# Slot scores of a gated-slot attention: one float32r pass over stacked split operands in place of two float32 half passes

## The chip, the cores and the metric

The kernel runs on one core of a Trainium2 chip. Its engines are TensorE (PE, matrix products; PEld is its weight load), VectorE (DVE), ScalarE (ACT), GpSimd (POOL) and SyncE (SP, which issues the transfers). The metric is device time in microseconds (us) of one execution.

## What is computed

A layer of four parts over x of shape 4 x 256 x 256 in float32: a causal attention, a feed-forward with int8 quantization, a second attention with 64 slots per head, and the feed-forward again, each on a layer norm of x and added to x. The change is in the second attention (16 heads, 128 wide). Its part that matters here:

```python
s = hs @ Ws1.T @ Ws2.T + bs2                # Ws1 16 x 256, Ws2 1024 x 16: rank 16
s = jnp.clip(s, -CLAMP, CLAMP).reshape(B, T, H, M).transpose(0, 2, 1, 3)
z = jax.lax.cumlogsumexp(s, axis=2)
es = jnp.exp(s)
enz = jnp.exp(-z)
...
A = jnp.where(mask, jnp.einsum('bhtd,bhjd->bhtj', q, k) * scale, 0.0)
ok = enz * jnp.einsum('bhtj,bhjm->bhtm', A, es)
qv = jax.nn.softmax(ok, axis=-1)
W2 = jnp.where(mask, jnp.einsum('bhtm,bhjm->bhtj', qv * enz, es), 0.0)
o = jnp.einsum('bhtj,bhjd->bhtd', W2, v)
```

## The kernel before

Each engine has its own program, written out by hand in the order in which it runs; semaphores (`wait_ge`, `then_inc`) tie them together, and an engine that waits holds up everything behind it in its program. The 1,024 tokens are four batches `b` of 256 (two tiles of 128). Heads go in eight pairs.

Products that need more than one rounded pass are split: a float32 operand becomes a float32r head (`_hi`, copied by ACT) and the float32r rest (`_lo`, subtracted by DVE or POOL), and three float32r passes take the place of a float32 product, which PE runs as two half passes. In the trace each half pass is a row of its own.

The scores of the slots come in two steps. At the head of the second attention `s1_product(b)` multiplies the 16 rows of Ws1 with the normalized tokens of batch `b` in float32, and ACT (`s1_copy`) brings the result out of PSUM into `s1`: 16 rows, with a row of ones at row 32 written by DVE (`BIAS_ROW`). Then there is one task "s" for each pair of heads and each half of the tokens, 16 in all: four products of `s1` (128 tokens as stationary operand) with 128 columns of `ws2` (16 rows of Ws2 and the bias in row 32). DVE clips the result (`b_clip_s`), ACT takes the exponential, and a sum over the tokens, a reciprocal and the later products follow.

The other tasks of a half are the projections q0, q1, k0, k1, the prefix sum z, the value and gate chunks c0 to c3, and the transposes et. In the loop (`b_body`, one pass per pair, four batches in each) PE puts them between the steps of the attention. For an even batch the order on PE is: transposes of the normalized slot weights `qp` (line 1554), task "s" (line 1453), W2 product (lines 1520 and 1523), q0, and so on. ACT, in the same place, runs the value copy and the tanh of chunk c3 (lines 697, 698), then copies the transposed weights to `zT` (line 727), on which the W2 product waits (`b_z`).

The second attention starts with a head part outside the loop. There DVE runs, one after the other: layer norm scaling of x, the two `tail`s that split x, the quantization of feed-forward tile 2 (`ffn_quant`: range, then rounding), the scaling of tile 3 and its quantization, the clip of the first slot scores, and more. PE runs in that part: transposes of x, `s1_product(0)` and `(1)`, the feed-forward transposes of tile 2, the first task "s". The products for batches 2 and 3 follow later in the head.

Of the kernel before, what the change touches and what calls it, by code (L numbers as in the profile page):

```python
# [38 lines left out]
P = 128  # L39
B, T, D = 4, 256, 256  # L40
HEADS = 16
# [5 lines left out]
HD = HEADS * P  # L47
M = 64
RANK = 16
BIAS_ROW = 32  # L50
SCALE = float(P) ** -0.5
MASKED = -1e10
LN_EPS = 1e-5
# [18 lines left out]
def layer_kernel(nc, x_in, a_wq, a_bq, a_wk, a_bk, a_wv, a_bv, a_wo, a_bo,  # L72
                 b_wq, b_wk, b_wv, b_wg, b_wo, b_ws1, b_ws2, b_bs2, b_gw,
                 f_w, f_ws, f_bias, consts, out):
    with ExitStack() as ctx:
# [3 lines left out]
        def sem(name):  # L79
            return ctx.enter_context(nc.semaphore(name))  # L80
# [52 lines left out]
        rinv = sb("rinv", [P, 2, 2])  # L133

        ws1 = sb("ws1", [P, C, RANK])
        s1 = sb("s1", [P, B * T])
        ws2 = sb("ws2", [P, HEADS * M])
        rot = sb("rot", [P, 2, HALF])
        rot_s = sb("rot_s", [P, 2, HALF])
        es_hi = sb("es_hi", [P, HALF], F32R)  # L140
# [3 lines left out]
        es = sb("es", [P, TILES, 2 * M])  # L144
        esT = sb("esT", [P, B * T])
        enz = sb("enz", [P, TILES, 2 * M])
        gt = sb("gt", [P, 2, 2 * P])
        G = bv_b[:, :].rearrange("p (t n) -> p t n", t=TILES)
        ok = sb("ok", [P, 2, 2, M])
# [38 lines left out]
        cast_done = sem("cast_done")  # L188
        gwh_done = sem("gwh_done")
        init_done = sem("init_done")  # L190
        ones_done = sem("ones_done")
        s1_ps, s1_done = sem("s1_ps"), sem("s1_done")
        out_st = sem("out_st")

        class Norm:
# [90 lines left out]
        def _(sp):  # L286
# [33 lines left out]
            sp.dma_start(ws1[:, :, :], b_ws1.rearrange("(c p) n -> p c n", p=P)).then_inc(small_ld, 16)  # L320
            sp.dma_start(gw[:, :], b_gw.rearrange("(p o) -> p o", o=1)).then_inc(small_ld, 16)

            sp.wait_ge(init_done, 3)
            sp.dma_start(ws2[0:RANK, :], b_ws2).then_inc(small_ld, 16)
            sp.dma_start(ws2[BIAS_ROW:BIAS_ROW + 1, :], b_bs2.rearrange("(o n) -> o n", o=1)).then_inc(small_ld, 16)
            sp.dma_start(const[:, K_TRI:K_END], consts[:, K_TRI:K_END]).then_inc(table_ld, 16)
            with sp.Fori(1, PAIRS) as i:
                cols = bass.ds(i * (2 * P), 2 * P)
# [32 lines left out]
        def _(pool):  # L361
            g = nc.gpsimd
            g.memset(minus_half[:, :], -0.5).then_inc(init_done, 1)
            g.memset(s1[:, :], 0.0).then_inc(init_done, 1)
            g.memset(ws2[:, :], 0.0).then_inc(init_done, 1)
            g.memset(wo_hi[:, :, :].bitcast(F32), 0.0)
            g.memset(wo_lo[:, :, :].bitcast(F32), 0.0)
            g.memset(oT_hi[:, 1, :, :].bitcast(F32), 0.0)
# [21 lines left out]
            def ffn_add(f, b):  # L390
# [17 lines left out]
            pool.wait_ge(bias_ld, 16 * 4)  # L408
            g.tensor_tensor(acc[:, :, :], acc[:, :, :], bo_b[:, :].unsqueeze(1).to_broadcast([P, TILES, D]), ALU.add
                            ).then_inc(a.y_acc, 1)  # L410
            with pool.Fori(0, PAIRS - 1) as i:
                split_tail(a, i + 1, 0)
                split_tail(a, i + 1, 1)
                split_out_tail(a, i, wo)
                split_tail(a, i + 1, 2)
# [103 lines left out]
        def _(act):  # L519
# [31 lines left out]

            def s1_copy(b):

                act.wait_ge(s1_ps, b + 1)
                s.activation(s1[0:RANK, b * T:(b + 1) * T], ps[0:RANK, ffns[0].banks[b], 0:T], ACT.Copy).then_inc(s1_done, 1)


            split_head(a, 0, 0)
# [79 lines left out]
            transposed(0, 2, 4)  # L638
            transposed(0, 3, 5)
            a_exp_step(0)  # L640
            act.wait_ge(small_ld, 16 * 7)
            s.activation(w8b[:, :, :], w8[:, :, :].bitcast(I8), ACT.Copy).then_inc(cast_done, 1)
            s.activation(gwh[:, :], gw[:, :], ACT.Copy, scale=0.5).then_inc(gwh_done, 1)
            with act.Fori(0, PAIRS - 1) as i:
                a_body(i, False)
            a_body(PAIRS - 1, True)
# [134 lines left out]
                        if nxt:  # L781
                            b_okexp_step(x + b + 1)

            act.wait_ge(init_done, 3)
            act.wait_ge(gwh_done, 1)
            for j, name in enumerate(B_TASKS[:-1]):
                b_task(0, 0, j, 0, 0)
# [19 lines left out]
        def _(dve):  # L807
# [19 lines left out]
            def tail(m, b, bank):  # L827

                cols = slice(b * T, (b + 1) * T)
                dve.wait_ge(xts[m].hi, b + 1)  # L830
                d.tensor_tensor(xT_lo[:, :, cols], ps[:, bank, :].rearrange("p (c t) -> p c t", c=C),
                                xT_hi[:, :, cols].bitcast(F32), ALU.subtract).then_inc(xts[m].lo, 1)

            def ffn_quant(f, b):
                ffn_range(f, b)
# [48 lines left out]
            ln_stats(0, 3, x_ld[3], 16)  # L884
            ln_scale(0, 2)
            ln_scale(0, 3)
            dve.wait_ge(init_done, 2)
            d.memset(s1[BIAS_ROW:BIAS_ROW + 1, :], 1.0).then_inc(ones_done, 1)

            def a_v(n, f, pair, half):  # L890

# [92 lines left out]
            for f in range(4):  # L984
                n = 4 + f
                a_v((n % 2, n // 2, n + 1), f, 0, 0)
                if f == 1:
                    tail(0, 2, 4)
                    a_norm_step(0)
                if f == 2:  # L990
                    tail(0, 3, 5)
            with dve.Fori(0, PAIRS - 1) as i:
                a_body(i, False)
            a_body(PAIRS - 1, True)
# [6 lines left out]
            ln_scale(1, 2)  # L1001
            tail(1, 0, ffns[0].banks[0])
            tail(1, 1, ffns[0].banks[1])
            ffn_quant(0, 2)
            ln_scale(1, 3)
            ffn_quant(0, 3)

# [191 lines left out]
            b_gate(n0(8), 0, 2, 0)  # L1199
            b_okn_max(0, 0, 0)  # L1200
            b_slots(0)
            b_recip(None, 0, 2)
            with dve.Fori(0, PAIRS - 1) as i:
                b_body(i, False)
            b_body(PAIRS - 1, True)
# [13 lines left out]
        def _(pe):  # L1219
# [34 lines left out]
            def s1_product(b):  # L1254

                pe.wait_ge(xts[1].lo, b + 1)
                for c in range(C):
                    ins = mm(ps[0:RANK, ffns[0].banks[b], 0:T], ws1[:, c, :], xT[:, c, b * T:(b + 1) * T],
                             start=(c == 0), stop=(c == C - 1))
                ins.then_inc(s1_ps, 1)  # L1260

# [164 lines left out]
            ffn_product(0, 1)  # L1426
            transpose_x(1, 0, ffns[0].banks[0])
            transpose_x(1, 1, ffns[0].banks[1])
            s1_product(0)
            s1_product(1)  # L1430
            ffn_transpose(0, 2)
            pe.wait_ge(s1_done, 2)
            pe.wait_ge(ones_done, 1)

            def b_free(i, h, j):

# [8 lines left out]
            def b_task(i, h, j, half, phase):  # L1445
                b_free(i, h, j)
                name, bank = B_TASKS[j], slot(i, h, j)[0]
                pair = i + h // 2
                n = (bank,)
                if name == "s":  # L1450
                    for t in range(HT):
                        tile = HT * half + t
                        ins = mm(PJ[bank][:, t * P:(t + 1) * P], s1[:, tile * P:(tile + 1) * P],
                                 ws2[:, bass.ds(pair * P, P)], start=True, stop=True)
                    ins.then_inc(b_.proj_ps, 1)
                elif name[0] in "qk":
                    proj_qk(b_, n, name, pair, half)
                elif name == "z":

                    pe.wait_ge(b_es_lo, phase + 1)  # L1460
                    by_tile = lambda ap: ap.rearrange("p (b t m) -> p b t m", b=2, t=2)
                    for part in (es_hi, es_lo):

                        mm(PJ[bank], sums[:, 0:P], part[:, :], start=(part is es_hi), stop=False)
                        ins = mm(by_tile(PJ[bank])[:, :, 1, :], sums[:, P:2 * P], by_tile(part[:, :])[:, :, 0, :],
                                 start=False, stop=(part is es_lo))
                    ins.then_inc(b_.proj_ps, 1)
                elif name == "et":
                    for t in range(HT):
                        ins = tr(PJ[bank][:, t * P:(t + 1) * P], es[:, HT * half + t, :], ident)  # L1470
                    ins.then_inc(b_.proj_ps, 1)
                else:

                    k = int(name[1])
                    if k == 0:
                        pe.wait_ge(b_.w_lo, pair * b_.splits + 3)
                    for c in range(C):
                        vg_chunk(bank, k, half, c)
# [230 lines left out]
```

## Time and profile before

| | |
|---|---|
| median of three runs | 822.16 us (821.42 to 823.87) |
| profiled execution | span 819.7 us from the first to the last instruction; its own time is not listed apart from the three |
| PE busy | 770.2 us, 94% of the span |
| DVE, ACT, POOL busy | 71%, 53%, 35% |
| chain that ended last | PE 90%, DVE 5% |
| the 128 half passes of the tasks "s" | 17.0 us of busy PE, mean 276 ns |

Rows of one engine overlap a little, since a matrix product is counted until its last result is out; the pace of a stream is read from the starts, or from the chain. The granted clock of PE is 1.00 at 2.4 GHz and 0.50 at 1.2 GHz.

### The profile page before, as it was taken

The page shows a single profiled execution, that of the slowest core. Times are in us where ns is not written, and L with a number is a line of the kernel's source. Part 1 is how long each engine was busy: PE and PEld are TensorE (multiplying, and loading weights), DVE is VectorE, ACT ScalarE, POOL GpSimd, SP SyncE. Part 2 cuts the span into 40 slices and gives each one's busy share as a digit, 9 for nine tenths or more (in the row PEclk, how much of TensorE's full clock was granted, in tenths as well). Part 3 has the DMA queues.
Part 4 walks back from the last instruction along what each step waited for, and adds up shares of the span by engine and source line. Part 5 has one row for each costly group of instructions (what it writes and reads, how often), then busy time and mean ns, then how long its engine had stood idle before and what let it go on. Part 6 is the DMA issues. An engine that isn't in the chain of part 4 may idle for free.

```text
span 819.7 us, 14465 instructions
## 1 busy us (share of the span) xinstructions
PE 770.2 (94%) x4556; PEld 654.7 (80%) x4556; DVE 581.3 (71%) x1502; ACT 435.4 (53%) x1188; POOL 285.7 (35%) x291
## 2 busy tenths in 40 slices
PE   5899999999999995799999999999999999999963
PEld 4788888888888883478888888888888888888852
DVE  4555555555555558878887888798879888887686
ACT  3555565555556542465556465656564665555420
POOL 6311020201102014444536346355364463553222
PEclk9999999999999999899999999999999999999997
DMA  6110101101010100100101001001010010000001
GB/s 226 40 52 13 38 13 38 51 0 51 13 38 13 51 1 14 53 0 14 54 0 54 10 13 51 0 13 51 0 33 31 13 51 0 13 0 0 1 1 52
DMA packets 23653, 23.74 MB, mean 29 GB/s; under 512 B 2369, under 2 KB 23361, under 8 KB 23506
## 3 DMA queue, kind: packets, MB, share of 16 engines
q1 hardware_dynamic: 23634, 23.51, 9.0%
q8 instruction: 10, 0.16, 0.1%
q14 instruction: 9, 0.07, 0.0%
HBM read 22.45 MB, written 1.05 MB: 29 GB/s over the span
## 4 chain that ended last, share of the span: by engine, by line
PE 90%; DVE 5%; POOL 1%; ACT 1%; issue 1%; DMA 1%; SPq 0%; DVEq 0%; ACTq 0%; POOLq 0%
PE ps L1276 22%; PE ps L1483 11%; PE ps L1385 7%; PE ps L1283 5%; PE ps L1306 5%; PE ps L1349 3%; PE ps L1390 3%; PE ps L1495 3%; PE ps L1520 3%; PE ps L1325 3%; PE ps L1507 2%; PE ps L1402 2%; PE ps L1537 2%; PE ps L1539 2%; PE ps L1509 2%; PE ps L1508 2%
## 5 line engine op out<-in xcount | busy, mean ns | idle before, releaser
L1276 PE MATMUL ps<-xT_hi,w_hi 128*128 128x512 f32 x256 | 110.4, 431 | 5.3 <-DVE rot L1012 3.6
L1276 PE MATMUL ps<-xT_hi,w_lo 128*128 128x512 f32 x256 | 102.0, 399 | 0.0
L1276 PE MATMUL ps<-xT_lo,w_hi 128*128 128x512 f32 x256 | 101.5, 396 | 0.0
L1042 DVE TENSOR_TENSOR wt<-ps,const 128x384 f32<-128x384 f32 x128 | 68.2, 554 | 40.4 <-PE ps L1496 20.4
L383 POOL TENSOR_TENSOR w_lo<-w_raw,w_hi 128x512 fp32r<-128x512 f32 x32 | 40.8, 1285 | 155.8 <-ACT w_hi L535 154.1
L439 POOL TENSOR_TENSOR rot_s<-rot_s,const 128x512 f32<-128x512 f32 x64 | 82.1, 1293 | 21.1 <-ACT rot_s L678 21.1
L580 ACT ACTIVATE wt<-wt,negmax 128x128 f32<-128x128 f32 (+1 forms) x128 | 56.7, 444 | 28.2 <-DVE negmax L906 28.2
L894 DVE TENSOR_TENSOR v<-ps,bv_b 128x256 f32<-128x256 f32 x64 | 27.0, 422 | 51.9 <-PE ps L1283 51.9
L697 ACT ACTIVATE v<-ps 128x256 f32<-128x256 f32 x64 | 24.5, 382 | 72.4 <-PE ps L1483 72.2
L1276 PEld LDWEIGHTS ps<-xT_hi,w_hi 128*128 128x128 f32 x256 | 49.0, 192 | 15.1 <-issue 4.5
L1031 DVE RECIPROCAL enz<-zs 128x128 f32<-128x128 f32 x64 | 60.3, 943 | 1.0 <-ACT zs L684 1.0
L459 POOL TENSOR_TENSOR qp<-oke,enz 128x256 f32<-128x256 f32 x32 | 23.6, 738 | 99.3 <-ACT oke L702 99.3
L1276 PEld LDWEIGHTS ps<-xT_hi,w_lo 128*128 128x128 f32 x256 | 48.9, 191 | 11.3
L901 DVE TENSOR_TENSOR wt<-ps,const 128x128 f32<-128x128 f32 x64 | 18.3, 286 | 55.1 <-PE ps L1306 55.1
L1483 PE MATMUL ps<-wc_hi,xT_hi 128*128 128x512 f32 x128 | 56.3, 440 | 0.0
L677 ACT ACTIVATE rot_s<-ps 64x512 f32<-64x512 f32 x64 | 38.1, 596 | 32.1 <-PE ps L1276 30.1
L1276 PEld LDWEIGHTS ps<-xT_lo,w_hi 128*128 128x128 f32 x256 | 49.3, 192 | 7.1
L1012 DVE TENSOR_TENSOR rot<-ps,const 128x512 f32<-128x512 f32 x64 | 43.6, 682 | 15.3 <-ACT rot_s L678 15.3
L597 ACT ACTIVATE wt<-ps 128x384 f32<-128x384 f32 x64 | 30.2, 487 | 38.6 <-PE ps L1325 38.6
L1483 PE MATMUL ps<-wc_hi,xT_lo 128*128 128x512 f32 x128 | 50.4, 394 | 0.0
L1483 PE MATMUL ps<-wc_lo,xT_hi 128*128 128x512 f32 x128 | 50.3, 393 | 0.0
L930 DVE TENSOR_TENSOR accT<-ps,accT 128x512 f32<-128x512 f32 x58 | 39.8, 686 | 11.9 <-PE ps L1390 10.8
(170 smaller groups left out, 2236.9 us busy)
## 6 DMA issues: line engine op xcount, KB each, us to landing
w_raw<-a_w_q SPq DMA_DIRECT2D x8, 256.0 KB, 2.8
w_raw<-a_w_k SPq DMA_DIRECT2D x8, 256.0 KB, 3.2
wv<-a_w_v SPq DMA_DIRECT2D x8, 256.0 KB, 3.4
wo<-a_w_o SPq DMA_DIRECT2D x8, 256.0 KB, 2.7
w_raw<-b_Wq SPq DMA_DIRECT2D x8, 256.0 KB, 2.7
w_raw<-b_Wk SPq DMA_DIRECT2D x8, 256.0 KB, 3.3
wc<-b_Wv SPq DMA_DIRECT2D x8, 256.0 KB, 3.5
wc<-b_Wg SPq DMA_DIRECT2D x8, 256.0 KB, 3.7
```

Of the source, the lines that this page charges most:

```text
L383: g.tensor_tensor(lo[:, :, :], raw[:, :, :], hi[:, :, :].bitcast(F32), ALU.subtract).then_inc(ph.w_lo, 1)
L439: g.tensor_tensor(ap, ap, const[:, col:col + T].unsqueeze(1).to_broadcast([P, 2, T]), ALU.mult).then_inc(b_rotmul, 1)
L580: last = s.activation(wt[:, h, lo:hi], wt[:, h, lo:hi], ACT.Exp, bias=negmax[:, h, r:r + 1], scale=(1.0, -1.0)[r], accum_out=rowsum[:, h, ...
L930: d.tensor_tensor(accT[:, c, cols], Y_, accT[:, c, cols], ALU.add).then_inc(ph.y_acc, 1)
L1012: d.tensor_tensor(rot[:, k, :].rearrange("p (b t) -> p b t", b=2), PJ[n[0]].rearrange("p (b t) -> p b t", b=2), const[:, col:col + T].unsq ...
L1031: d.reciprocal(enz[:, HT * half + k, :], zs[:, k * P:(k + 1) * P]).then_inc(b_recip_done, 1)
L1042: d.tensor_tensor(dst, src[:, 0:384], tri3, ALU.mult).then_inc(done, 1)
L1276: ins = mm(PJ[n[0]], w[:, m, c, h * P:(h + 1) * P], x[:, c, cols], start=(t == 0), stop=(t == len(terms) - 1))
L1283: ins = mm(bank_ap, x[:, c, cols], w[:, c, :], start=(t == 0), stop=(t == len(terms) - 1))
L1306: ins = mm(W_[h][:, lo:hi], qT[:, h, t0 + r * P:t0 + (r + 1) * P], kT[:, h, t0:t0 + hi - lo], start=True, stop=True)
L1385: mm(Y_, w[:, h, c * P:(c + 1) * P], oT_hi[:, half, h, :], start=(h == 0 and w is wo_hi), stop=False)
L1483: ins = mm(PJ[bank], x[:, c, tile], w[:, c, :], start=(c == 0 and t == 0), stop=(c == C - 1 and t == 2))
```

## The change

Both operands of the task "s" are split into head and rest and stacked along the contraction, in three groups of 32 rows: `ws2s` holds head, head, rest of Ws2 and bias, `s1s` holds head, rest, head of the first step. One float32r product over 96 rows then sums the three partial products that otherwise were three passes.

- `s1_product` multiplies with `ws1x`, which holds Ws1 three times (96 columns, zeros between), so that its result stands three times in PSUM. ACT copies all 96 rows to float32r and adds a column `s1_one` (one at the bias rows) on the way. Then DVE subtracts the heads from the middle group (`s1_tail`), four times in the kernel.
- `ws2` is laid in the space of `enz`. Three transfers bring Ws2, two the bias. ACT copies 96 x 1024 to `ws2s`, and DVE subtracts in the last group, both ahead of the loop of the first attention.
- POOL fills one buffer less with zeros, and copies Ws1 three times into `ws1x`. DVE's row of ones goes.

```diff
-            sp.wait_ge(init_done, 3)
-            sp.dma_start(ws2[0:RANK, :], b_ws2).then_inc(small_ld, 16)
-            sp.dma_start(ws2[BIAS_ROW:BIAS_ROW + 1, :], b_bs2.rearrange("(o n) -> o n", o=1)).then_inc(small_ld, 16)
+            sp.wait_ge(init_done, 2)
+            for g in range(S_ROWS // S_GROUP):
+                sp.dma_start(ws2[g * S_GROUP:g * S_GROUP + RANK, :], b_ws2).then_inc(ws2_ld, 16)
+            for g in (0, 2):
+                row = g * S_GROUP + RANK
+                sp.dma_start(ws2[row:row + 1, :], b_bs2.rearrange("(o n) -> o n", o=1)).then_inc(ws2_ld, 16)
...
-            g.memset(s1[:, :], 0.0).then_inc(init_done, 1)
-            g.memset(ws2[:, :], 0.0).then_inc(init_done, 1)
+            g.memset(ws2[0:S_ROWS, :], 0.0).then_inc(init_done, 1)
+            g.memset(ws1x[:, :, :], 0.0).then_inc(ws1x_zero, 1)
...
+            g.tensor_tensor(s1_one[:, :], ident[:, RANK:RANK + 1], ident[:, 2 * S_GROUP + RANK:2 * S_GROUP + RANK + 1],
+                            ALU.add).then_inc(ws1x_done, 1)
+            pool.wait_ge(small_ld, 16 * 5)
+            pool.wait_ge(ws1x_zero, 1)
+            for r in range(S_ROWS // S_GROUP):
+                g.tensor_copy(ws1x[:, :, r * S_GROUP:r * S_GROUP + RANK], ws1[:, :, :]).then_inc(ws1x_done, 1)
...
+                act.wait_ge(ws1x_done, 1)
                 act.wait_ge(s1_ps, b + 1)
-                s.activation(s1[0:RANK, b * T:(b + 1) * T], ps[0:RANK, ffns[0].banks[b], 0:T], ACT.Copy).then_inc(s1_done, 1)
+                s.activation(s1s[0:S_ROWS, b * T:(b + 1) * T], ps[0:S_ROWS, ffns[0].banks[b], 0:T], ACT.Identity,
+                             bias=s1_one[0:S_ROWS, 0:1]).then_inc(s1_hi, 1)
...
+            act.wait_ge(ws2_ld, 16 * 5)
+            s.activation(ws2s[0:S_ROWS, :], ws2[0:S_ROWS, :], ACT.Copy).then_inc(ws2_hi, 1)
...
+            def s1_tail(b):
+                rows, cols = slice(S_GROUP, 2 * S_GROUP), slice(b * T, (b + 1) * T)
+                dve.wait_ge(s1_hi, b + 1)
+                d.tensor_tensor(s1s[rows, cols], ps[rows, ffns[0].banks[b], 0:T], s1s[rows, cols].bitcast(F32),
+                                ALU.subtract).then_inc(s1_done, 1)
...
-            d.memset(s1[BIAS_ROW:BIAS_ROW + 1, :], 1.0).then_inc(ones_done, 1)
...
+            dve.wait_ge(ws2_hi, 1)
+            d.tensor_tensor(ws2s[low, :], ws2[low, :], ws2s[low, :].bitcast(F32), ALU.subtract).then_inc(ws2_done, 1)
...
-            ffn_quant(0, 2)
+            ffn_range(0, 2)
+            s1_tail(0)
+            s1_tail(1)
+            ffn_round(0, 2)
...
             b_slots(0)
+            s1_tail(2)
             b_recip(None, 0, 2)
+            s1_tail(3)
...
-                    ins = mm(ps[0:RANK, ffns[0].banks[b], 0:T], ws1[:, c, :], xT[:, c, b * T:(b + 1) * T],
+                    ins = mm(ps[0:S_ROWS, ffns[0].banks[b], 0:T], ws1x[:, c, :], xT[:, c, b * T:(b + 1) * T],
...
-                        ins = mm(PJ[bank][:, t * P:(t + 1) * P], s1[:, tile * P:(tile + 1) * P],
-                                 ws2[:, bass.ds(pair * P, P)], start=True, stop=True)
+                        ins = mm(PJ[bank][:, t * P:(t + 1) * P], s1s[0:S_ROWS, tile * P:(tile + 1) * P],
+                                 ws2s[0:S_ROWS, bass.ds(pair * P, P)], start=True, stop=True)
```

PE still waits for four counts of `s1_done` ahead of its loop, and for two ahead of the first task "s"; `s1_done` is now counted by DVE's subtraction.

At the head, DVE's program before, between the split of x and the rounding of feed-forward tile 2 (`amax`, `qsc`, `qrs` are the range, `qm`, `qb` the rounding):

```order
L831 TENSOR_TENSOR xT_lo<-ps,xT_hi 128x2x256 [waits xt1_hi] x2
L841 TENSOR_REDUCE amax<-xn 128x2 [waits ln1_xn]
L843 TENSOR_SCALAR qsc<-amax 128x2 [waits f0_amax]
L845 RECIPROCAL qrs<-qsc 128x2 [waits f0_sc]
L854 TENSOR_SCALAR qm<-xn,qrs 128x256 [waits f0_qb,f0_rs]
```

and the same place of the change:

```order
L850 TENSOR_TENSOR xT_lo<-ps,xT_hi 128x2x256 [waits xt1_hi] x2
L867 TENSOR_REDUCE amax<-xn 128x2 [waits ln1_xn]
L869 TENSOR_SCALAR qsc<-amax 128x2 [waits f0_amax]
L871 RECIPROCAL qrs<-qsc 128x2 [waits f0_sc]
L857 TENSOR_TENSOR s1s<-ps,s1s 32x256 [waits s1_hi] x2
L880 TENSOR_SCALAR qm<-xn,qrs 128x256 [waits f0_qb,f0_rs]
```

Two subtractions that wait for ACT's copies now stand ahead of the rounding and of all that follows on DVE.

At the end of the head, just ahead of the loop (`oksum` and `okeps` are `b_slots`, `enz` the reciprocal), DVE's program before:

```order
L1058 TENSOR_TENSOR oke<-ok,okmax 128x256
L1074 TENSOR_REDUCE oksum<-oke 128x4
L1077 SCALAR_TENSOR_TENSOR okeps<-oksum 128x4
L1031 RECIPROCAL enz<-zs 128x128
L1203 UNCONDITIONAL_BRANCH
```

and of the change:

```order
L1088 TENSOR_TENSOR oke<-ok,okmax 128x256
L1104 TENSOR_REDUCE oksum<-oke 128x4
L1107 SCALAR_TENSOR_TENSOR okeps<-oksum 128x4
L857 TENSOR_TENSOR s1s<-ps,s1s 32x256
L1061 RECIPROCAL enz<-zs 128x128
L857 TENSOR_TENSOR s1s<-ps,s1s 32x256
L1235 UNCONDITIONAL_BRANCH
```

A subtraction now stands on either side of the reciprocal, and the branch into the loop behind the second.

## Rows read from the trace of the kernel before

**Rows 1.** The page: busy time of each engine, and the chain by engine.

```profile
PE 770.2 (94%) x4556; PEld 654.7 (80%) x4556; DVE 581.3 (71%) x1502; ACT 435.4 (53%) x1188; POOL 285.7 (35%) x291
...
PE 90%; DVE 5%; POOL 1%; ACT 1%; issue 1%; DMA 1%; SPq 0%; DVEq 0%; ACTq 0%; POOLq 0%
```

**Rows 2.** Stretches: length, busy PE, PEld, DVE, ACT, POOL, granted clock, DMA, GB/s.

```profile
327.00:330.00 3.00, 2.81 (x7) 0.96 (x8) 2.24 (x7) 1.12 (x3) 0.16 (x1) 0.50 0.00 0
...
344.00:347.00 3.00, 2.81 (x7) 2.29 (x8) 3.00 (x8) 0.00 (x0) 0.92 (x3) 0.55 0.01 3
...
360.00:745.00 385.00, 384.43 (x2349) 326.88 (x2348) 319.15 (x656) 225.83 (x623) 185.98 (x183) 1.00 0.07 21
```

**Rows 3.** Timeline in the loop, even batch: start, duration, engine, what [idle before <-releaser].

```profile
387.11 0.38 PE L1554 MATMUL ps<-const,qp 128*128 128x128 f32 x2
...
387.32 1.06 PE L1453 MATMUL ps<-ws,s 128*128 x8
387.38 0.39 ACT L697 ACTIVATE v<-ps 128x256 f32<-128x256 f32 x1 [1.86 <-PE ps L1483]
...
387.93 0.39 ACT L727 ACTIVATE zT<-ps 128x256 f32<-128x256 f32 x1
...
388.37 0.30 PEld L1520 LDWEIGHTS ps<-zT,esT 64*128 64x128 f32 x4 [0.18 <-ACT zT L727]
...
388.42 0.69 DVE L1025 TENSOR_SCALAR clip_buf<-ps 128x512 f32<-128x512 f32 x1
```

**Rows 4.** Timeline, the last such place, where no task "s" is left.

```profile
776.69 0.38 PE L1554 MATMUL ps<-const,qp 128*128 128x128 f32 x2
...
777.87 0.70 PE L1520 MATMUL ps<-zT,esT 64*128 64x256 f32 x4 [0.81 <-ACT zT L727]
```

**Rows 5.** Chain in order of time: start, length, what.

```profile
387.49 0.89 PE ps L1453 x8
...
395.14 0.12 PE ps L1465
...
396.66 0.22 PE ps L1508 x2
```

**Rows 6.** Timeline of the head, first place.

```profile
327.19 3.59 PE L1258 MATMUL ps<-xT,ws 128*16 128x256 f32 x8 [0.56 <-DVE xT_lo L831]
...
329.11 0.37 ACT L555 ACTIVATE s<-ps 16x256 f32<-16x256 f32 x1 [1.36 <-PE ps L1258]
...
329.50 0.61 DVE L854 TENSOR_SCALAR qm<-xn,qrs 128x256 f32<-128x256 f32 x2
...
330.81 0.37 ACT L555 ACTIVATE s<-ps 16x256 f32<-16x256 f32 x1 [1.33 <-PE ps L1258]
...
334.18 0.63 ACT L666 ACTIVATE es<-clip_buf 128x512 f32<-128x512 f32 x1 [2.44 <-DVE clip_buf L1025]
```

**Rows 7.** Group: busy, mean ns of one | idle before, releaser.

```profile
L894 DVE TENSOR_TENSOR v<-ps,bv_b 128x256 f32<-128x256 f32 x64 | 27.0, 422 | 51.9 <-PE ps L1283 51.9
```

**Rows 8.** Timeline at the entry of the second attention's loop, by engine.

```profile
358.83 0.94 DVE L1031 RECIPROCAL enz<-zs 128x128 f32<-128x128 f32 x1
...
359.52 0.38 PE L1554 MATMUL ps<-const,qp 128*128 128x128 f32 x2
...
360.36 0.39 ACT L727 ACTIVATE zT<-ps 128x256 f32<-128x256 f32 x1
...
360.88 0.70 PE L1520 MATMUL ps<-zT,esT 64*128 64x256 f32 x4
```

**Rows 9.** Timeline at the start, ahead of the first attention's loop, by engine.

```profile
24.62 1.93 DVE L915 TENSOR_SCALAR wt<-wt,rinv 128x128 f32<-128x128 f32 x4
...
28.34 0.49 ACT L597 ACTIVATE wt<-ps 128x384 f32<-128x384 f32 x1 [3.60 <-PE ps L1325]
...
32.11 0.29 DVE L901 TENSOR_TENSOR wt<-ps,const 128x128 f32<-128x128 f32 x1 [4.29 <-PE ps L1306]
...
34.95 0.99 DVE L915 TENSOR_SCALAR wt<-wt,rinv 128x128 f32<-128x128 f32 x4
```

More of the change, by code:

```diff
@@ L49 @@
 RANK = 16
-BIAS_ROW = 32
+S_ROWS = 96
+S_GROUP = 32
 SCALE = float(P) ** -0.5
@@ L135, in layer_kernel @@
         ws1 = sb("ws1", [P, C, RANK])
-        s1 = sb("s1", [P, B * T])
-        ws2 = sb("ws2", [P, HEADS * M])
+        ws1x = sb("ws1x", [P, C, S_ROWS])
+        s1_one = sb("s1_one", [P, 1])
+        s1s = sb("s1s", [P, B * T], F32R)
+        ws2s = sb("ws2s", [P, HEADS * M], F32R)
         rot = sb("rot", [P, 2, HALF])
@@ L146, in layer_kernel @@
         enz = sb("enz", [P, TILES, 2 * M])
+        ws2 = enz[:, :, :].rearrange("p t m -> p (t m)")
         gt = sb("gt", [P, 2, 2 * P])
@@ L190, in layer_kernel @@
         init_done = sem("init_done")
-        ones_done = sem("ones_done")
-        s1_ps, s1_done = sem("s1_ps"), sem("s1_done")
+        ws2_ld, ws2_hi, ws2_done = sem("ws2_ld"), sem("ws2_hi"), sem("ws2_done")
+        ws1x_zero, ws1x_done = sem("ws1x_zero"), sem("ws1x_done")
+        s1_ps, s1_hi, s1_done = sem("s1_ps"), sem("s1_hi"), sem("s1_done")
         out_st = sem("out_st")
@@ L410, in _ @@
                             ).then_inc(a.y_acc, 1)
+            pool.wait_ge(const_ld, 16)
+            g.tensor_tensor(s1_one[:, :], ident[:, RANK:RANK + 1], ident[:, 2 * S_GROUP + RANK:2 * S_GROUP + RANK + 1],
[4 more added lines that the diff above has]
+                g.tensor_copy(ws1x[:, :, r * S_GROUP:r * S_GROUP + RANK], ws1[:, :, :]).then_inc(ws1x_done, 1)
             with pool.Fori(0, PAIRS - 1) as i:
@@ L640, in _ @@
             a_exp_step(0)
-            act.wait_ge(small_ld, 16 * 7)
+            act.wait_ge(small_ld, 16 * 5)
             s.activation(w8b[:, :, :], w8[:, :, :].bitcast(I8), ACT.Copy).then_inc(cast_done, 1)
             s.activation(gwh[:, :], gw[:, :], ACT.Copy, scale=0.5).then_inc(gwh_done, 1)
+            act.wait_ge(ws2_ld, 16 * 5)
+            s.activation(ws2s[0:S_ROWS, :], ws2[0:S_ROWS, :], ACT.Copy).then_inc(ws2_hi, 1)
             with act.Fori(0, PAIRS - 1) as i:
@@ L782, in b_body @@
                             b_okexp_step(x + b + 1)
-            act.wait_ge(init_done, 3)
             act.wait_ge(gwh_done, 1)
@@ L886, in _ @@
             ln_scale(0, 3)
-            dve.wait_ge(init_done, 2)
-            d.memset(s1[BIAS_ROW:BIAS_ROW + 1, :], 1.0).then_inc(ones_done, 1)
             def a_v(n, f, pair, half):
@@ L991, in _ @@
                     tail(0, 3, 5)
+            low = slice(2 * S_GROUP, S_ROWS)
+            dve.wait_ge(ws2_hi, 1)
+            d.tensor_tensor(ws2s[low, :], ws2[low, :], ws2s[low, :].bitcast(F32), ALU.subtract).then_inc(ws2_done, 1)
             with dve.Fori(0, PAIRS - 1) as i:
@@ L1428, in _ @@
             transpose_x(1, 1, ffns[0].banks[1])
+            pe.wait_ge(ws1x_done, 4)
             s1_product(0)
@@ L1432, in _ @@
             pe.wait_ge(s1_done, 2)
-            pe.wait_ge(ones_done, 1)
+            pe.wait_ge(ws2_done, 1)
             def b_free(i, h, j):
```

## The prediction

> **What bounds the kernel now.** I read the page first: TensorE (PE) is busy 94% of the span and makes 90% of the chain that ended last, VectorE (DVE) 5% [rows 1]. Then the table by stretches, because that share is a mean: in the loop of the second attention PE is busy 384.43 of 385 us at the full clock, while at the head of the second attention it runs at half the clock and is not what ends last [rows 2]. So there are two questions: is the slot pass on PE's path inside the loop, and what do the added steps cost at the head, where another engine leads.
>
> For the first I read the timeline at one pass of the loop [rows 3]. The reader is to see two things that run side by side behind the transposes of the slot weights at 387.11. On PE the slot pass starts at 387.32 and its eight half passes take 0.89 us by the chain [rows 5], so PE could go on at about 388.21. On ScalarE (ACT) the value copy starts at 387.38, behind the end of task c3, then the tanh, then the copy of the transposed weights, zT, from 387.93 to 388.32. The W2 product needs zT, and its weight load starts at 388.37, 0.05 us behind the copy, after a wait of 0.18 put down to ACT. The slot pass is already the shorter of the two branches. The other 14 slot tasks behind such transposes look alike; the widest distance from transposes to product is 360.88 - 359.52 = 1.36 [rows 8]. And the trace makes an experiment by itself [rows 4]: the last time that these transposes come there is no slot task left, PE sits idle for 0.81 us until zT, and from the transposes to the product it still takes 777.87 - 776.69 = 1.18 us, against 388.37 - 387.11 = 1.26 us with the whole slot pass in between.
>
> **The loop, term by term.** Half of a slot task goes: four passes for eight. No row shows a float32r pass of 128 columns. From below, the float32r pass of 256 columns takes 0.12 us, so one of 128 takes at most that if it streams at the same rate; a float32 half pass of only 64 columns takes 0.22 / 2 = 0.11 us, the same as one of 128 columns (0.89 / 8), so the weight load sets a floor of about 0.11 [rows 5]. From above, a pass that costs as much as the pair that it replaces takes 0.22. I take 0.11, since both near rows stand there: a task takes 4 x 0.11 = 0.45 us in place of 0.89, 0.44 less, and over 16 tasks that is 7.1 us of PE time. What of it shows in the end is what zT leaves, 1.26 - 1.18 = 0.08 us for half of the tasks and 1.36 - 1.18 = 0.18 at most for the others; and it is ACT that is a little later there (its value copy depends on c3, not on the slot pass). I take **0**, with 7 x 0.08 + 8 x 0.18 = 2.0 us of gain as the far end. Behind the slot pass waits the clip on DVE, but that starts at 388.42, after the gate, when the old pass was already done [rows 3]; an earlier pass starts no earlier chain.
>
> **The head, first place.** DVE gets two subtractions between the range and the rounding of feed-forward tile 2. The second can only run when ACT has copied the scores of tile 1, and that copy starts at 330.81, when PE leaves the eight half passes of the two products (3.59 us at half clock) [rows 2, 6]. With 0.37 for the copy it ends at 331.18; 0.06 for the hand-over and 0.42 for the subtraction (the row of a 128x256 addition out of PSUM [rows 7]; I give 32 partitions no discount) give 331.66, less 0.08 by which neighbours on DVE overlap: 331.6. The rounding stood at 329.50. So everything queued behind it on DVE comes **2.1 us** later: the rounding, the transposes of tile 2 that stand ahead of the slot pass on PE, the normalization and quantization of tile 3, and the clip, on which ACT waits 2.44 us before the exponentials at 334.18 [rows 6]. DVE has no gap there that could take it up. The slot pass itself, 0.44 shorter, sits in front of a clip that is two microseconds off, and gives nothing. The bounds: 0.7 if only the two subtractions counted, 2.3 with a slower copy and the wider weight load (96 columns for 16).
>
> **The head, second place.** DVE gets one subtraction before and one after the reciprocal that starts at 358.83, and PE now waits for the second before it enters the loop. 358.83 + 0.42 + 0.94 + 0.42, less two overlaps of 0.08, is 360.45; with the hand-over PE starts the transposes at 360.5 instead of 359.52 [rows 7, 8]. The W2 product moves by less, because ACT is no longer busy when they arrive: transposes 0.38, zT 0.39, hand-overs 0.1 to 0.15 make 361.4 to 361.5 against 360.88. I take **0.6 us**; ends 0.4 and 1.0 (the whole of PE's wait). From there PE has no idle time to give it back.
>
> **The start.** The split of the second weights is a copy of 1,024 columns on ACT (twice the 0.63 of the exponential, so about 1.2 us) and a subtraction on DVE (twice the clip, 1.3 us). ACT then has 3.60 us and DVE 4.29 us of idle time ahead of the loop's first work [rows 3, 6, 9], so both are hidden; without that cover they would cost 2.5 us together. Three more transfers on SP stand behind the loads that the first tasks need, and two memsets' worth of work leaves POOL and DVE where they were waiting anyway: 0. Left are four small POOL operations right behind its long addition at 21 to 26 us. DVE's four scalings at 24.62 take 1.93 us beside that addition and 0.99 without it [rows 9], and they are on PE's path; POOL busy a little longer may cost some of the rest. I take **0.2 us**, between 0 and 0.5.
>
> Sum: 0 + 2.1 + 0.6 + 0.2 = 2.9 us. It is made on the profiled execution, span 819.7 us, 2.5 below the median of the three times; as a difference it is added to that median: 822.16 + 2.9 = **825.1 us**.
>
> **Rivals.**
> *The saving lands.* If zT followed the slot pass more than I read, the loop gives 7.1 us and the head takes 2.9: 818.0. For it speaks that the chain of waits names the slot pass, 0.89 us [rows 5]; against it the idle PE in [rows 4]. It decides if the product starts with the end of the slot pass wherever zT is ready. The Trainium skill (TensorE: Matmul & The Clock Gate, Back-to-back issue gap) gives about 81 ns for one pass of 128 columns in a stream with weight loads; no run here shows it for float32r. By that figure, as an estimate, a task would take 0.32 us, the saving would be 9.1 and the end 816.0; by my reading it changes nothing, since ACT sets the end.
> *The new pass is no faster* (0.22 each). Then PE's time stays, and so does the total, 825.1 to 825.3. It goes together with the forecast.
> *The products at the head run at the full clock* in the timed runs. In the trace the granted clock is 0.50 there, the lower level of 1.2 GHz, after PE had stood nearly idle [rows 2]. At 2.4 GHz the second product takes half of 1.8 us, the copy starts 0.9 earlier, and the first place costs 1.2: 824.2.
> *The clock later in the head.* From 344 to 347 PE is busy 2.81 of 3 us at 0.55 [rows 2]; at the full clock that work takes 1.4 less. With everything shifted by 2 us, the fall may not come: 2.9 - 1.4 = 1.5, 823.7. Or, as PE has less to do while DVE waits, another stretch of this size falls to the half level: 2.9 + 1.4 = 4.3, 826.5. The same page (Part 1) says that the gate's timing does not start with the kernel; a single trace cannot show that, but it would make these two differ from run to run.
>
> **Chances and range.** Forecast, with the slow new pass: 0.50. Products at full clock: 0.20. No fall at 344: 0.13. A further fall: 0.12. The saving lands: 0.05. What a measurement of this kernel can tell from no change is 0.3%, 2.5 us, so the line is at 824.6. The forecast lies only 0.4 above it; nine tenths of its chance and the further fall are above: 0.57. The two milder cases and the rest of the forecast are within: 0.38. Faster: 0.05. The forecast alone runs from 824.0 (a little gain in the loop) to 826.2. For 8 in 10 I go from 822.3, below the milder cases with their own spread, to 827.2, above the further fall.
>
> **What would show it.** Right: in the loop the slot pass shrinks from eight rows to four at about 0.11, PE's busy time falls by about 7 us, and PE stands idle about 0.4 us more ahead of each W2 product, released by zT; the distance from transposes to product stays 1.2 to 1.4; the loop's period stays. At the head DVE idles about 1.3 us between the first and the second subtraction, released by ACT, and the clip starts 2.1 later behind the last normalization; before the loop PE waits about 1 us for DVE. Wrong: a shorter distance from transposes to product; a clip that comes in its old place; an early part that moved by more than half a microsecond.

## The result, and the profile after

The changed kernel takes 827.87 us (median of 6 runs, 827.21 to 828.46); the kernel before took 823.29 beside it (6 runs, 821.42 to 826.13). The ratio is 1.0053, 95% interval 1.0034 to 1.0071: slower by 2.8 to 5.8 us. The forecast was 825.1 with a range from 822.3 to 827.2: the direction came as forecast, and the time lies 0.67 us above the range. The profile of the change is of the slowest of its six executions (828.46), so the spans of the two profiles, 819.71 and 826.65, lie further apart than the medians.

The page of the changed kernel answers to [rows 1]: PE is busy 3.9 us less, where about 7 was forecast (6.4 of it are there in the loop, below; outside the loop PE is busy longer), and its share of the chain falls from 90% to 88%.

```profile
PE 766.3 (93%) x4492; PEld 651.7 (79%) x4492; DVE 584.1 (71%) x1506; ACT 436.7 (53%) x1189; POOL 285.7 (35%) x295
...
PE 88%; DVE 6%; ACT 3%; issue 1%; POOL 1%; DMA 1%; ACTq 0%; SPq 0%; DVEq 0%; POOLq 0%
```

The two profiled executions are compared between the same events in each, so that what is late at one place doesn't count again at the next:

| from | to | before | after | difference | forecast |
|---|---|---|---|---|---|
| start of the trace | first s1 product | 327.19 | 327.92 | +0.73 | +0.2 |
| first s1 product | rounding of tile 2 | 2.31 | 4.59 | +2.28 | +2.1 |
| rounding | clip of the first slot scores | 3.88 | 3.99 | +0.11 | 0 |
| clip | copy of the slot sums on ACT | 5.88 | 7.21 | **+1.33** | 0 |
| copy of the sums | first W2 product of the loop | 21.62 | 22.64 | +1.02 | +0.6 |
| first W2 product | first slot-weight transposes of the last pass | 384.54 | 384.98 | +0.44 | 0 |
| those transposes | end | 74.29 | 75.32 | +1.03 | 0 |
| whole span | | 819.71 | 826.65 | +6.94 | +2.9 |

The first row comes from a transfer of x at the very start (the head of the chain is 5.03 us of "DMA acc<-x" after, 4.14 before, and 2.82 to 4.84 in the runs below; whether the change has a part in it, single profiles do not say). The last lies behind everything that the change touches, and in the eleven profiles told of here that stretch takes 73.86 to 76.28. Without these two the difference is 5.18 us, inside the measured 2.8 to 5.8.

The loop, in the timeline at the place of [rows 3] (start, duration, engine, what, idle before and releaser):

```profile
392.65 0.38 PE L1587 MATMUL ps<-const,qp 128*128 128x128 f32 x2
392.78 0.64 PE L1486 MATMUL ps<-ws2s,s1s 96*128 x4
392.93 0.38 ACT L717 ACTIVATE v<-ps 128x256 f32<-128x256 f32 x1 [1.90 <-PE ps L1516]
...
393.47 0.39 ACT L747 ACTIVATE zT<-ps 128x256 f32<-128x256 f32 x1
...
393.91 0.30 PEld L1553 LDWEIGHTS ps<-zT,esT 64*128 64x128 f32 x4 [0.63 <-ACT zT L747]
393.91 0.70 PE L1553 MATMUL ps<-zT,esT 64*128 64x256 f32 x4 [0.48 <-ACT zT L747]
393.95 0.68 DVE L1055 TENSOR_SCALAR clip_buf<-ps 128x512 f32<-128x512 f32 x1
```

Eight rows have become four, the wait of the product's weight load for zT has grown from 0.18 [rows 3] to 0.63 us, by the 0.45 that the pass got shorter, and from transposes to product it still takes 393.91 - 392.65 = 1.26 us, the distance of before. Nothing of the saving shows. In one stretch of the loop of equal length, PE of the changed kernel is busy 363.15 of 370 us, where [rows 2] have it busy 99.9% of the time:

```profile
370.00:740.00 370.00, 363.15 (x2194) 307.56 (x2194) 306.88 (x631) 217.36 (x599) 181.18 (x177) 1.00 0.07 22
```

The first place of the head, in the timeline, beside [rows 6]:

```profile
327.92 3.54 PE L1290 MATMUL ps<-xT,ws1x 128*96 128x256 f32 x8 [0.65 <-DVE xT_lo L850]
...
330.52 0.42 DVE L857 TENSOR_TENSOR s1s<-ps,s1s 32x256 fp32r<-32x256 f32 x1 [0.41 <-ACT s1s L572]
331.56 0.47 ACT L572 ACTIVATE s1s<-ps,s_one 96x256 fp32r<-96x256 f32 x1 [1.07 <-PE ps L1290]
332.06 0.42 DVE L857 TENSOR_TENSOR s1s<-ps,s1s 32x256 fp32r<-32x256 f32 x1 [1.13 <-ACT s1s L572]
332.51 0.61 DVE L880 TENSOR_SCALAR qm<-xn,qrs 128x256 f32<-128x256 f32 x2
...
333.64 0.40 PE L1273 MATMUL ps<-ident_bf,qb 128*128 128x128 bf16 x4 [2.18 <-DVE qb L884]
```

DVE stands idle 1.13 us in front of the second subtraction, for ACT, which in turn waits for PE. The rounding and all behind it are late, and PE waits 2.18 us for them. What follows on PE is the piece that the forecast lacked. The row of the stretch right behind, first of the kernel before:

```profile
334.50:341.50 7.00, 5.19 (x24) 3.39 (x22) 5.72 (x9) 4.41 (x9) 6.16 (x4) 1.00 0.46 151
```

then of the changed kernel, with six products there by the chain (start, length, what):

```profile
334.50:341.50 7.00, 6.01 (x21) 4.13 (x22) 5.55 (x12) 3.11 (x6) 4.44 (x3) 0.51 0.19 55
```

```profile
337.13 2.67 PE ps L1308 x6
```

The granted clock is 0.51 there, 1.2 GHz, and six projection passes take 2.67 us; six of the same line take 1.39 us at 2.4 GHz elsewhere in this trace. Before, this part of the program ran at the full clock. From the clip to the copy of the sums, before

```profile
333.38 0.68 DVE L1025 TENSOR_SCALAR clip_buf<-ps 128x512 f32<-128x512 f32 x1
...
339.26 0.60 ACT L684 ACTIVATE zs<-ps 128x512 f32<-128x512 f32 x1
```

and in the change:

```profile
336.50 0.69 DVE L1055 TENSOR_SCALAR clip_buf<-ps 128x512 f32<-128x512 f32 x1
...
343.71 0.60 ACT L704 ACTIVATE zs<-ps 128x512 f32<-128x512 f32 x1
```

it takes 5.88 and 7.21 us, the 1.33 of the table.

The second place, by the timeline, beside [rows 8]:

```profile
363.27 0.42 DVE L857 TENSOR_TENSOR s1s<-ps,s1s 32x256 fp32r<-32x256 f32 x1
...
363.72 0.95 DVE L1061 RECIPROCAL enz<-zs 128x128 f32<-128x128 f32 x1
...
364.70 0.42 DVE L857 TENSOR_TENSOR s1s<-ps,s1s 32x256 fp32r<-32x256 f32 x1
365.36 0.43 PE L1587 MATMUL ps<-const,qp 128*128 128x128 f32 x2 [1.64 <-DVE s1s L857]
...
366.35 0.70 PE L1553 MATMUL ps<-zT,esT 64*128 64x256 f32 x4
```

PE waits 1.64 us for the second subtraction before it may enter the loop, and the product follows 0.99 us behind the transposes, not 1.36.

### The profile page after: what moved, and what is told of

Its sections match the earlier page's. It is cut to its first block, busy times and chain, and to the rows that moved or that the text cites. A ratio compares the mean times of both kernels' runs of the same rounds, so it can differ in the third digit from the quotient of the medians.

```text
span 826.7 us, 14355 instructions
## 1 busy us (share of the span) xinstructions
PE 766.3 (93%) x4492; PEld 651.7 (79%) x4492; DVE 584.1 (71%) x1506; ACT 436.7 (53%) x1189; POOL 285.7 (35%) x295
## 4 chain that ended last, share of the span: by engine, by line
PE 88%; DVE 6%; ACT 3%; issue 1%; POOL 1%; DMA 1%; ACTq 0%; SPq 0%; DVEq 0%; POOLq 0%
PE ps L1308 22%; PE ps L1516 10%; PE ps L1417 7%; PE ps L1315 5%; PE ps L1338 5%; PE ps L1381 3%; PE ps L1422 3%; PE ps L1528 3%; PE ps L1553 3%; PE ps L1357 2%; PE ps L1434 2%; PE ps L1540 2%; PE ps L1570 2%; PE ps L1572 2%; PE ps L1571 2%; PE ps L1542 2%
```

## The experiments

The theory was: the saving is lost to zT; the two subtraction places cost what is measured above; and the half clock of 334.6 to 341.4 comes from PE standing idle behind the s1 products. The rivals were that the longer pass was on the path after all, that the loop pays for something else in the change, and that the clock falls whatever PE does. The numbers below are medians; the kernel before was run beside each.

**The change with the old pass length (e1).** The same stacked operands, multiplied as float32, eight half passes again:

```diff
-  ins = mm(PJ[bank][:, t * P:(t + 1) * P], s1s[0:S_ROWS, tile * P:(tile + 1) * P],
-           ws2s[0:S_ROWS, bass.ds(pair * P, P)], start=True, stop=True)
+  ins = mm(PJ[bank][:, t * P:(t + 1) * P], s1s[0:S_ROWS, tile * P:(tile + 1) * P].bitcast(F32),
+           ws2s[0:S_ROWS, bass.ds(pair * P, P)].bitcast(F32), start=True, stop=True)
```

> The change with all its preparation, but the task s as two float32 half passes over the same stacked operands. Theory (zT sets the W2 product in the loop, so the length of the slot pass gives nothing): the same time as the changed kernel within 0.5 us, about 827.9 us; from the transposes to the W2 product still 1.26 and 1.36 us, PE idle ahead of the product back to about 0.2. Rival (the shorter pass did save its 7 us in the loop and the head cost far more): about 834 to 835 us.

828.17 us (826.36 to 828.62; before 822.74), ratio 1.0062 (1.0042 to 1.0082), the change's own. The pass is as long as before, 17.0 us over 128 half passes in place of 10.3 over 64, and the time is that of the short pass.

**The shorter pass alone (e2).** The kernel before, with `s1` and `ws2` rounded to float32r and no rests, one pass, no subtraction:

```diff
-        s1 = sb("s1", [P, B * T])
-        ws2 = sb("ws2", [P, HEADS * M])
+        s1 = sb("s1", [P, B * T], F32R)
+        ws2s = sb("ws2s", [P, HEADS * M], F32R)
...
+            s.activation(ws2s[:, :], ws2[:, :], ACT.Copy).then_inc(ws2_hi, 1)
...
-                                 ws2[:, bass.ds(pair * P, P)], start=True, stop=True)
+                                 ws2s[:, bass.ds(pair * P, P)], start=True, stop=True)
```

> The kernel before with the task s as one float32r pass over unsplit, rounded operands; no subtractions, no wider products, so the head stays as it was. It leaves out the rest parts of both operands. Theory: the same as before within 0.5 us (823.3), with 0.45 us more idle PE ahead of each W2 product. Rival (the saving lands and the head hides it in the change): 7 us faster, about 816.

822.4 us (819.53 to 825.64; before 822.74), ratio 0.9991 (0.9975 to 1.0008). From the first W2 product to the last pass it takes 384.53 us, against 384.54 before. In the 370 us below PE is busy 6.4 us less than in the same stretch of before, where it was 369.51:

```profile
370.00:740.00 370.00, 363.11 (x2197) 307.93 (x2196) 308.06 (x632) 216.72 (x599) 178.93 (x176) 1.00 0.07 22
```

With e1 this settles the loop from both sides: eight passes or four, the loop lasts as long.

**The first place moved (e3).** Both subtractions go behind the quantization of tile 2 and the range of tile 3, where ACT's copies are done:

```diff
-            ffn_range(0, 2)
+            ffn_quant(0, 2)
+            ln_scale(1, 3)
+            ffn_range(0, 3)
             s1_tail(0)
             s1_tail(1)
-            ffn_round(0, 2)
-            ln_scale(1, 3)
-            ffn_quant(0, 3)
+            ffn_round(0, 3)
```

> The change with the two subtractions of the first place moved behind the range of tile 3, where ACT's copies are done. Theory: the clip comes 0.8 us later than before instead of 2.3, and PE stays at the full clock from 331 to 341, which gives back 1.4 more: about 3 us less than the change, 825 us. Rival A (the clock falls there anyway, since PE still waits for the first slot scores): only 1.5 less, 826.4. Rival B (the wait is not on the path): no change, 827.9.

824.1 us (822.81 to 825.6), ratio 1.002 (1.0008 to 1.0032). The rounding of tile 2 is back in its place, 2.22 us behind the products. On DVE the subtractions wait for nobody:

```profile
332.21 0.17 DVE L871 RECIPROCAL qrs<-qsc 128x2 f32<-128x2 f32 x1
332.40 0.75 DVE L857 TENSOR_TENSOR s1s<-ps,s1s 32x256 fp32r<-32x256 f32 x2
333.19 0.61 DVE L880 TENSOR_SCALAR qm<-xn,qrs 128x256 f32<-128x256 f32 x2
```

They cost their own 0.75 us: from rounding to clip it takes 4.77 in place of 3.99. From clip to copy of the sums it takes 6.38, between the 5.88 of before and the 7.21 of the change. Together 2.42 us less than the change by the trace. From the copy to the first W2 product it takes another 1.15 less (21.49 for 22.64): the half-clock stretch that the change has from 348 to 352 us (0.57) is not in this profile (1.00). The medians differ by 3.8 and the ratios by 0.0033, or 2.7 us.

Rival A is not refuted by this. PE still waits as long as in the change, now ahead of the slot pass, and the clock falls behind it, for a shorter stretch: 0.81 from 334.5 to 341.5, between the 1.00 of before and the 0.51 of the change.

```profile
333.21 0.68 PE L1486 MATMUL ps<-ws2s,s1s 96*128 96x128 f32 x4 [2.15 <-DVE s1s L857]
```

**PE kept busy behind the s1 products (e4).** Five products of 512 columns into a bank that nobody reads stand where PE waited:

```diff
             s1_product(1)
+            for _ in range(5):
+                mm(ps[:, 2, :], xT_hi[:, 0, 0:P], xT_hi[:, 0, 0:HALF], start=True, stop=True)
             ffn_transpose(0, 2)
```

> The change with five extra products of 512 columns on PE behind the second product of the head, into a bank that nobody reads, so that PE works while DVE waits. Theory (PE's idle time there lets the clock fall, and that costs 1.4 us beside the wait itself): granted clock 1.00 from 334 to 341, first sums and reciprocal 1.3 to 1.4 us earlier, time about 826.5. Rival (the fall has nothing to do with this idle time): clock 0.50 there as in the change, 827.9 or a little more.

828.3 us (828.22 to 829.57), ratio 1.0075 (1.0055 to 1.0094). The step that the experiment is about came as the theory says: full clock, and 5.88 us from clip to copy, 1.33 less. But the total did not follow in any of the six executions. Behind the wait ahead of the loop, where the change has 1.00, the clock is now down:

```profile
334.50:341.50 7.00, 4.90 (x28) 3.34 (x25) 6.51 (x12) 3.75 (x7) 5.33 (x3) 1.00 0.24 78
362.00:370.00 8.00, 7.04 (x36) 6.07 (x37) 4.27 (x8) 4.12 (x12) 1.73 (x2) 0.79 0.00 0
```

From the first W2 product to the last pass it takes 386.35, 1.37 more than in the change, and the end 0.96 more. So in this trace the gain at one place was given back at the next one where PE stands and waits. The wait alone does not explain it: the same 1.64 us stand there in the change and in e3, with the clock at 1.00 behind them. Either PE's waits bring the clock down in some executions, or a fall that is covered at one place comes at another; e9 takes this wait away as well.

**The second place moved (e5).** Both subtractions ahead of the reciprocal, and PE's wait moved behind the transposes, to the first task "s" of the loop, which needs it:

```diff
             s1_tail(2)
-            b_recip(None, 0, 2)
             s1_tail(3)
+            b_recip(None, 0, 2)
...
                         if rest:
+                            pe.wait_ge(s1_done, 4)
                             b_task(i, 1 + b // 2, B_TASKS.index("s"), half, phase)
...
-            pe.wait_ge(s1_done, 4)
             with pe.Fori(0, PAIRS - 1) as i:
```

> The change with both subtractions of the second place ahead of the reciprocal, and PE's wait for them moved behind the transposes of the first pass through the loop. Theory (PE's wait of 1.6 us there costs 0.9 us net): from the first slot-weighted product (b_ok) to the first W2 product about 6.9 us in place of 7.7, as before the change; time about 827 us. Rival (the wait is hidden, since ACT is busy with c3 then): 7.7 us still, time 828.

826.49 us (824.38 to 829.35; before 823.5), ratio 1.003 (1.0014 to 1.0045). The transposes no longer wait, and what PE waits for stands ahead of the slot pass, in the time of zT:

```profile
362.64 0.38 PE L1587 MATMUL ps<-const,qp 128*128 128x128 f32 x2
...
363.38 0.66 PE L1486 MATMUL ps<-ws2s,s1s 96*128 x4 [0.36 <-DVE s1s L857]
363.47 0.39 ACT L747 ACTIVATE zT<-ps 128x256 f32<-128x256 f32 x1
...
363.99 0.70 PE L1553 MATMUL ps<-zT,esT 64*128 64x256 f32 x4
```

From the product of `A` and `es` (L1540 to L1542) to the first W2 product it takes 6.30 us; in the change 7.73, before 6.82. The whole cost of the second place goes, and half a microsecond more.

**Both together (e9): e4 and e5 in one.** With the wait ahead of the loop gone there is nothing left behind which the clock of e4 fell.

> The change with both: five spare products of 512 columns behind the second s1 product (into a bank that nobody reads), and the subtractions of the second place ahead of the reciprocal with PE's wait moved behind the transposes. Theory (the clock falls because PE stands waiting for DVE, once behind the s1 products and once ahead of the loop): neither fall comes, so the stretch from the clip to the copy of the sums is 5.9 as with the spare products alone, and the stretch from the last of the W2 normalization to the first W2 product 6.3 as with the second place alone; the total is that of the second place alone, 826.5, less 1.4: about 825.1. Rival (the falls are only put off, PE gets one somewhere else for each that is covered): another half-clock stretch shows between 340 and 370 or in the tail, and the total stays at 826.5 or above.

824.29 us (823.1 to 825.79; before 821.88), ratio 1.0018 (1.0001 to 1.0036). Neither of the two falls is there:

```profile
334.50:341.50 7.00, 4.64 (x25) 3.41 (x26) 6.62 (x10) 4.71 (x8) 6.19 (x4) 1.00 0.41 126
...
362.00:370.00 8.00, 8.00 (x54) 6.95 (x51) 5.60 (x13) 5.37 (x15) 4.88 (x5) 1.00 0.00 0
```

From clip to copy it takes 5.88 where e5, which differs only by the five products, takes 7.25; from the product of `A` and `es` to the first W2 product 6.30 us again. So the trace gives the clock term 1.37 us, as the theory had it. The rival asked for a half-clock stretch elsewhere. The one between 344 and 352 us (0.79) is in the change and in the kernel before as well. But the end of the kernel, from the last pass on, takes 75.22 us, 1.17 more than in e5, with a clock of 0.94 from 740 to 800 us where e5 has 0.97; that a fall was put off to there is not excluded by these two traces. The total stays below the 826.5 of the rival. The times lean the same way: 0.0012 less by the ratios, or 1.0 us; 0.6 us if each median is set against that of the kernel before beside it (2.41 and 2.99). The intervals overlap, and the times alone would not show it. Each execution also has its mean granted clock: it is 0.977 or less in 6 of the 12 of e5 and in 1 of the 12 of e9, which leans the same way.

**Both places moved (e6).** The edits of e3 and e5:

> Both subtractions moved, at the first place and at the second. Theory: what the first place gave (3.8 us, 824.1) and what the second gives add up, about 823.2 us, so the same as before within its spread. Rival (they share a cause, the low clock, and do not add): 824 us.

823.02 us (820.72 to 825.35; before 823.5), ratio 0.9995 (0.9982 to 1.0009). The change is then worth nothing and costs nothing, to within the interval (1.5 us less to 0.7 us more): what made it slower is where its four subtractions stand, not that they are there. Its other parts together cost nothing that shows.

**The freed time filled (e7), and the same filling without the change (e8).** A projection is six passes. e7 is e6 with three passes of one ahead of the W2 product for batches 0 and 2, and three ahead of the o product for batch 0; the other halves stay behind, so no work is added. In the cut, `part(j, p)` runs half `p` of projection `j`; its definition and the loop's other lines are left out. e8 is the kernel before with the same filling.

```diff
+                        part(1 + b // 2, 0)
                         b_w2_product(x, b, i)
-                        if rest:
+                        if b == 0:
+                            part(1, 1)
+                        elif rest:
                             b_task(i, 1 + b // 2, B_TASKS.index("q0"), half, phase)
...
+                        if b == 0:
+                            part(2, 0)
                         b_o_product(x, b, i, last)
-                        if rest:
-                            b_task(i, 1 + b // 2, B_TASKS.index("q1"), half, phase)
+                        part(2, 1)
```

> The kernel with both subtractions moved, and half of a projection put into PE's idle time between the short slot pass and the W2 product: for batch 0 the first half of q0 goes ahead of the W2 product and the first half of q1 ahead of the o product, for batch 2 the first half of q1 goes ahead of the W2 product. Theory (the saved 0.45 us per task is there as idle PE time in front of zT and can be used): 15 places by 0.45 to 0.65 us, 6 to 9 us less than without, so 814 to 817 us. Rival (another wait, the masks or the rotations on DVE, ends last as soon as PE is faster): less than 2 us, 821 or more.

> The kernel before with the same move of half projections, but with the old slot pass of 0.89 us. Theory: there is only 0.1 to 0.3 us of idle PE time ahead of the W2 product to fill, so at most 15 x 0.2 = 3 us of gain, and the product comes 0.4 later: 820 to 823 us, clearly above the refilled kernel with the short pass. Rival (the gain comes from the new order alone and needs no shorter pass): the same gain as there, 814 to 817.

e7: 815.67 us (814.11 to 818.35), ratio 0.9893 (0.9874 to 0.9913). e8: 821.04 us (820.03 to 823.15), ratio 0.9971 (0.9956 to 0.9985). In e7 PE is busy without a gap again, with work that it had to do anyway; the timeline between transposes and W2 product shows where the passes went:

```profile
370.00:740.00 370.00, 370.00 (x2244) 311.90 (x2245) 314.19 (x647) 219.78 (x605) 182.81 (x179) 1.00 0.07 22
```

```profile
388.99 0.38 PE L1589 MATMUL ps<-const,qp 128*128 128x128 f32 x2
389.13 0.64 PE L1488 MATMUL ps<-ws2s,s1s 96*128 x4
389.61 0.45 PE L1309 MATMUL ps<-xT_hi,w_hi 128*128 128x512 f32 x1
389.89 0.40 PE L1309 MATMUL ps<-xT_lo,w_hi 128*128 128x512 f32 x1
390.12 0.39 PE L1309 MATMUL ps<-xT_hi,w_lo 128*128 128x512 f32 x1
390.44 0.70 PE L1555 MATMUL ps<-zT,esT 64*128 64x256 f32 x4
```

The loop (first W2 product to last pass) takes 377.26 us in e7 and 385.04 in e6, 7.8 less. Of that, 384.54 - 382.85 = 1.7 come from the order alone, as e8 shows beside the kernel before; the other 6.1, near the 6.4 of PE time that the short pass frees there, come only together with it. The distances say why: from the transposes to the W2 product it takes 1.45 us in e7 and 1.90 in e8, where the long pass leaves no room for the filling. Of all the kernels run this is the fastest, ahead of both kernels of the comparison.

## Why the prediction was wrong in size and right in direction

**The loop: right.** zT sets the product (e1, e2), at 1.26 us for the even half and 1.36 for the other, as [rows 3, 8] had it. The new pass takes 0.45 / 4 = 0.11 us by the chain, the value taken from the floor of the near rows:

```profile
365.80 0.45 PE ps L1486 x4
```

The Trainium skill (TensorE: Matmul & The Clock Gate, Back-to-back issue gap) has about 81 ns for such a pass; the trace does not agree for float32r, and the measurement decides. The change's loop is 0.44 us longer than that of before, e1's 0.23, e2's not at all; so it isn't the shorter pass, and which other part of the change it is stays open.

**The head, first place: mechanism right, 2.39 in place of 2.1.** The copy of 96 rows with a bias takes 0.47, not the 0.37 of the 16 rows before; and DVE's neighbours, which I let overlap by 0.08, stand 0.03 apart here. The two products ran at the half clock, as in the trace of before (0.50 from 327 to 331 us); the rival that had them at the full clock did not come in this profile.

**The head, second place: mechanism right, 0.91 in place of 0.6, and the wait itself was undersized.** By the distance from the product of `A` and `es`: 7.73 - 6.82. The transposes moved by 1.28, not 1.0 (from the first subtraction to them 2.09 us, not 1.67: two gaps of 0.03 where I let rows overlap, and 0.24 from DVE's end to PE's start, where I had 0.05); they gave back 0.37 between themselves and the product, as reckoned. PE waits 1.64 us there, not about 1: it comes 0.52 us earlier than before, for a reason that the forecast did not have (last section). Against e5, which has that gain and not the wait, the second place costs 7.73 - 6.30 = 1.43 us; that 0.91 lies so near to 0.6 is in part luck.

**The start: wrong, and small.** DVE's four scalings take 1.96 us beside POOL, 1.93 before; the two operations on the second weights are hidden as said.

**The step that failed is "The clock later in the head".** The forecast, at 0.50, took the clock as the trace of before had it, and gave "another stretch of this size falls to the half level" 0.12, at 1.4 us and 826.5. That rival is what happened in the trace: 1.33 us. The paragraph had this case in it, "as PE has less to do while DVE waits", and the first place had just been worked out to make PE wait two microseconds longer right behind a stretch at 0.50; it should have been weighed as a likely case, not as one of the least. With 1.33 for the clock and the two sizes above, the sum is 2.39 + 0.91 + 1.33 + 0.44 + 0.11 (between the copy of the sums and the second place) = 5.18 in place of 2.9. Of the 2.77 us between 825.1 and 827.87, 1.13 is no term of the sum at all: the kernel before had a median of 822.16 in the three runs that the sum was added to, and 823.29 in those beside the change. The range had the further fall within it; the 0.67 us by which the time lies above it are less than these 1.13.

The executions fit a clock term. The mean granted clock is 0.977 in all six of the change, and in the 69 of the kernel before that were run beside the experiments it is 0.977 or less in 18. Those at 0.985 (15) take 821.2 us in the mean, those at 0.977 (17) 825.1: the time of the kernel before moves with the clock too. The six of the change take 827.8, so at the same mean clock it is 2.7 us slower, near the 2.9 of the sum without a clock term, and the other 1.9 of the 4.6 go with the clock. A mean over an execution does not say where the clock was low.

What is not settled is when the clock falls. Behind PE's waits of 2.18 and 2.19 us in the first place it is at the half level from about 334 to 341 us (the change, e1, e5). Where the five products leave waits of 0.96 to 1.19 us (e4, e9), and in the kernel before (0.69) and e8 (0.93), it stays at 1.00 there. But e3 and e6 wait 2.15 us and have a shorter fall (0.81 and 0.76 from 334.5 to 341.5); e2, where PE waits 1.18 us for the rounding since its slot pass is shorter, has one too (0.71 from 331 to 334.5); and in e7, whose first place is that of e6, the clock stood at 0.50 from 324.5 to 338.2 without a break. So the length of the wait alone does not set the fall. That PE's waiting is the cause is supported by e4 and e9, where work in place of the wait takes the fall away at that place, and is not shown beyond that.

## What to carry to other kernels

A pass that is made shorter inside a window that another engine ends gains nothing until other work of the same engine is moved into that window: here the same change was worth nothing in place and, with the two costly places moved and the window filled, 1.1%, of which the filling alone gives 0.3% (e8). An operation that waits for another engine belongs in an in-order program where its input is already there; four subtractions of 0.42 us cost 3.3 us by where they stood, without the clock, and moved by a few lines nothing that a measurement could tell. And when a step makes PE idle in a part where its clock is already low, price the next stretch at the half clock too, and do not give that case the smallest chance.

## What the runs showed of the hardware

A float32 product with 96 columns as weights took less of PE's time here than the same product with 16. At the full clock, two such products and the four prefix sums between them take 358.03 - 355.51 = 2.52 us before, and 361.99 - 359.98 = 2.01 us in the change (2.52 in e2 and e8 too, which have 16 columns, and 2.00 to 2.01 in e1, e3, e5, e6 and e9, which have 96). At the half clock, in the first place, there is nearly no difference: 3.59 and 3.54 us for eight half passes. The row of the weight load behind it shows the difference as idle time for which the profile names no releaser, in the kernel before

```profile
358.03 0.19 PEld L1483 LDWEIGHTS ps<-wc_hi,xT_hi 128*128 128x128 f32 x1 [0.42 <-issue]
```

and not in the change:

```profile
361.96 0.19 PEld L1516 LDWEIGHTS ps<-wc_hi,xT_hi 128*128 128x128 f32 x1
```

What sets the idle time is not shown. In the change itself most of this half microsecond only lengthens PE's wait at the second place, since DVE ends last there; where that wait is gone it shows: e5 is 0.52 us faster there than the kernel before.
